# Own tiles in single buffers between long ones, x on ScalarE's queue, and g shared between two engines

## The reference

```
h   = concat([q1, q2]) @ w5 + b5                    # 300 wide
f6  = h @ w6 + b6
g   = (v @ v.T)[iu, ju]                             # all 44850 pairs i < j
f7  = (h[:, iu] * h[:, ju] * g) @ w7 + b7           # w7 is 44850 x 300
out8 = concat([f6, f7]) @ w8 + b8
y   = einsum('bu,bku->bk', out8, label_embedding)   # 200 label rows a sample
```

## Time and profile before

| | us |
|---|---|
| median of 3 runs (lowest, highest) | 1834.8 (1830.94, 1834.85) |
| the profiled execution | 1836.85 |
| its span | 1835.0 |
| PE busy | 1587.0 |
| DVE busy | 1479.3 |
| ACT busy | 921.9 |

### The profile page before, as it was taken

One profiled execution on the slowest core, in us unless ns is written; L12 is line 12 of the kernel. 1 busy time (PEld: TensorE's weight loads), 2 busy tenths in 40 slices (PEclk: granted clock), 3 DMA queues, 4 the chain that ended last, 5 costly groups with the idle time before them and its releaser, 6 DMA issues.

```text
span 1835.0 us, 24651 instructions
## 1 busy us (share of the span) xinstructions
PE 1587.0 (86%) x6936; PEld 1148.7 (63%) x6936; DVE 1479.3 (81%) x5519; ACT 921.9 (50%) x2851; POOL 33.3 (2%) x62
## 2 busy tenths in 40 slices
PE   0659999999999999997999999999999999989300
PEld 0236676777777777774777777767777777656200
DVE  8988987764699999978899987748777677498996
ACT  4443375765564646463564634434444444200798
POOL 0000000000000000000000000000000000000000
PEclk9789999999999999998999999999999999999755
DMA  7568966768789899997989999999999899899996
GB/s 283 230 262 317 368 261 247 270 216 287 290 310 419 324 401 368 384 338 303 403 306 414 344 401 409 369 304 386 353 341 344 318 387 356 273 420 421 359 417 246
DMA packets 139214, 616.99 MB, mean 336 GB/s; under 512 B 16432, under 2 KB 43693, under 8 KB 106181
## 3 DMA queue, kind: packets, MB, share of 16 engines
q1 hardware_dynamic: 105157, 368.24, 53.0%
q10 hardware_dynamic: 31744, 244.16, 34.4%
q0 software_dynamic: 2176, 3.01, 0.5%
HBM read 611.55 MB, written 3.79 MB: 335 GB/s over the span
## 4 chain that ended last, share of the span: by engine, by line
PE 71%; DVE 8%; DMA 8%; ACT 7%; SPq 3%; issue 2%; ACTq 0%; POOL 0%; DVEq 0%; POOLq 0%
PE bank L603 64%; ACT stream L753 6%; DMA wring<-in_w7p 5%; DVE junk L830 3%; PE bank L555 3%; DVE stream L946 2%; SPq L442 2%; PE bank L568 2%; DMA sring<-hrows 1%; DVE cring L928 1%; DVE cring L916 1%; ACT absjunk L669 1%; DMA stream<-in_x 1%; PE bank L544 0%; PE bank L614 0%
## 5 line engine op out<-in xcount | busy, mean ns | idle before, releaser
L603 PE MATMUL bank<-wring,cring 128*128 128x300 f32 (+1 forms) x5616 | 1451.6, 419 | 55.9 <-DVE cring L928 19.4
L603 PEld LDWEIGHTS bank<-wring,cring 128*128 128x128 f32 (+1 forms) x5616 | 1065.7, 191 | 424.4 <-DVE cring L916 30.5
L744 ACT ACTIVATE wring<-wring,gcol 128x300 f32<-128x300 f32 x1237 | 564.7, 532 | 613.3 <-DMA wring<-in_w7p 317.9
L946 DVE SCALAR_TENSOR_TENSOR stream<-stream,out 128x300 f32<-128x300 f32 x1335 | 546.0, 465 | 0.8 <-DMA stream<-in_label 0.4
L928 DVE TENSOR_TENSOR cring<-lefts,sring 128x1024 f32<-128x1024 f32 (+2 forms) x309 | 368.1, 1192 | 184.7 <-PE bank L603 182.2
L830 DVE SCALAR_TENSOR_TENSOR junk<-stream,ubc 128x300 bf16<-128x300 f32 x896 | 364.0, 465 | 10.4 <-DMA stream<-in_x 10.4
L669 ACT ACTIVATE absjunk<-stream 128x300 bf16<-128x300 f32 x448 | 196.1, 440 | 44.6 <-PE bank L603 42.6
L555 PE MATMUL bank<-stream,wts 128*32 128x300 f32 x896 | 66.2, 451 | 58.4 <-DVE small L872 58.4
L753 ACT ACTIVATE stream<-stream 128x300 f32<-128x300 f32 x265 | 115.5, 438 | 0.1
L946 DVE DVE_READ_ACCUMULATOR stream<-stream,out 128x1 f32 x1335 | 108.9, 82 | 0.0
L916 DVE SCALAR_TENSOR_TENSOR cring<-lefts,gcol,sring 128x128 f32<-128x128 f32 x334 | 95.0, 345 | 16.0 <-PE bank L603 14.8
(11 more groups left out here) (66 smaller groups left out, 241.3 us busy)
## 6 DMA issues: line engine op xcount, KB each, us to landing
stream<-in_label SPq DMA_DIRECT2D x320, 750.0 KB, 8.2
wring<-in_w7p ACTq DMA_DIRECT2D x184, 1200.0 KB, 8.4
stream<-in_x SPq DMA_DIRECT2D x64, 1050.0 KB, 12.3
sring<-hrows SPq DMA_DIRECT2D x152, 256.0 KB
wring<-in_w7p ACTq DMA_DIRECT2D x9, 1050.0 KB, 9.1
wring<-in_w7p ACTq DMA_DIRECT2D x9, 600.0 KB, 7.7
lefts<-hrows SPq DMA_DIRECT2D x48, 64.0 KB, 6.8
sring<-hrows SPq DMA_DIRECT2D x32, 88.0 KB
```

Of the source, the lines that this page charges most:

```text
L603: mm = pe.matmul(acc[b % 4][:, 0:E], cring[0:rows, p % CSLOTS, b % 2, j0 + j, :], w, start=(p == BEGIN[b] and j == 0), stop=(p == END[b] - ...
L744: ins = nc.scalar.activation(w, w, ACT.Copy, scale=gcol[:, t:t + 1])
L946: ins = nc.vector.scalar_tensor_tensor(out=row_in, in0=row_in, scalar=1.0, in1=out8[:, m % 4, :], op0=ALU.mult, op1=ALU.mult, accum_out=sc ...
```

## The change

- `unit_table` takes an order of buffers, `ORDER`. The own tiles become five units (2, 2, 2, 2 and 1 tiles), each in one buffer: the right operands in places 0 and 1, the left ones in places 2 and 3. They stand singly among A, D and B buffers. A cycle is 93 units over 24 buffers; `SHIFT` is 42. The last tile (50 rows) is now unit 74 (`SHORT`). `tile_rows` follows, so the columns of `w7p` are laid out anew.
- An own buffer is loaded by 10, 6, 6, 6 and 10 copies for each batch tile (26 in all before, 38 now).
- Single stages: of a unit's tiles, `folded(p)` (two of four, two of three, one of two, none of one) still get g on DVE, one instruction each; the others are one DVE product, and ACT scales their w7 rows. ACT's scaling therefore runs at every position. PE waits for it always.
- x loads that replace x of steps 2 and later are issued by ACT, at position `DOTS[s][1] + 5`, after `softexp` and ahead of the position's `w7_load` and `w7_scale`. Those that replace step 0 and step 1 stay on SP; those of step 1 go out at position 0, behind `s_load(0)`, `left_load(0)` and `s_load(1)` (before: position -13).
- `DOTS` is moved: step 3 has positions 0 to 18 (before -6 to 6), steps 4 and 5 end at 34 and 50 (before 24 and 43), the later ones follow. `EARLY_ROWS` goes from 65 to 80, so the tail has 64 chunks instead of 67. `STORED` goes from 5 to 7.

```
-CUSTOM = (4, 4, 1)
+CUSTOM = (2, 2, 2, 2, 1)
+ORDER = (("A", 0), ("A", 1), ("D", 0), ("A", 2), ("own", 0), ("A", 3), ("D", 1), ("A", 4), ("own", 1), ("A", 5),
+         ("D", 2), ("A", 6), ("own", 2), ("A", 7), ("own", 3), ("B", 0), ("B", 1), ("own", 4)) + tuple(
+             ("B", k) for k in range(2, NB))
...
-    SHIFT = next(k for k, u in enumerate(UNITS) if u[1] == 6)
+    SHIFT = FIRST_USE[KINDS.index(("A", 5))]
...
+    def folded(p):
+
+        n = UNITS[p % NU][3]
+        return 0 if len(live(p)) == 2 or n == 1 else min(2, n - 1)
...
-    DOTS = [(-34, -27), (-27, -20), (-20, -6), (-6, 6), (6, 24), (24, 43), (43, 54), (54, 65), (65, 77), (77, 89),
-            (100, 114), (123, 137), (146, 160), (169, 183), (192, 206), (215, 229)]
+    DOTS = [(-34, -27), (-27, -20), (-20, -4), (0, 18), (18, 34), (34, 50), (50, 60), (60, 70), (70, 80), (80, 92),
+            (105, 119), (128, 142), (151, 165), (174, 188), (197, 211), (220, 234)]
...
-    X_FREE = 7
-    STORED = 5
+    X_FREE = 5
+    L_FREE = 8
+    STORED = 7
...
-    EARLY_ROWS = 65
+    EARLY_ROWS = 80
...
+    def x_free(s):
+        return 0 if s == 1 else DOTS[s][1] + X_FREE
...
+        def x_load(queue, n):
+            if X_BEFORE[n] is not None:
+                queue.wait_ge(x_used, X_BEFORE[n] // PARTS + 1)
+            queue.dma_start(xring[:, X_SLOT[n]], x_v[n]).then_inc(x_in[X_SLOT[n]], 16)
...
-                for n in [n for n in range(XSLOTS, NS * PARTS) if DOTS[X_BEFORE[n] // PARTS][1] + X_FREE == q]:
-                    x_load(n)
                 if q == 0:
                     s_load(0)
                     left_load(0)
-                    for n in range(1, SSLOTS):
+                    s_load(1)
+                for n in [n for n in range(XSLOTS, NS * PARTS) if x_free(X_BEFORE[n] // PARTS) == q]:
+                    if X_BEFORE[n] < 2 * PARTS:
+                        x_load(sp, n)
+                if q == 0:
+                    for n in range(2, SSLOTS):
                         s_load(n)
...
-                if SHIFT <= p < SHIFT + BOTH:
-                    pe.wait_ge(w7_ready, p - SHIFT + 1)
-                else:
+                pe.wait_ge(w7_ready, p + 1)
+                if folded(p):
                     pe.wait_ge(w7_in[n_block % WSLOTS], 16 * (n_block // WSLOTS + 1))
...
-                for t in range(UNIT_TILE[u], UNIT_TILE[u + 1]):
+                for t in range(UNIT_TILE[u], UNIT_TILE[u + 1] - folded(p)):
...
+                for n in [n for n in range(XSLOTS, NS * PARTS) if x_free(X_BEFORE[n] // PARTS) == q]:
+                    if X_BEFORE[n] >= 2 * PARTS:
+                        x_load(act, n)
                 if 0 <= q < POS:
                     if q in FROM and FROM.index(q) + 2 < len(BLOCKS):
                         w7_load(FROM.index(q) + 2)
-                    if SHIFT <= q + AHEAD < SHIFT + BOTH:
+                    if q + AHEAD < POS:
                         w7_scale(q + AHEAD)
...
-                    for j in range(j0, j0 + n):
+                    b, whole = tiles[0], n - folded(p)
+                    for j in range(j0 + whole, j0 + n):
...
+                    nc.vector.tensor_tensor(cut(cring, p % CSLOTS, j0, whole), in0, cut(sring, nb % SSLOTS, j0, whole),
+                                            ALU.mult).then_inc(c_ready, 1)
```

More of the change, by code:

```diff
@@ L93, in tile_rows @@
     left[28:50], right[28:50] = 2 * P + np.arange(22), 2 * P + np.arange(22) + 22
-    tiles.append((left, right))
+    own.append((left, right))
+    tiles = []
+    for left, buf, j0, n in UNITS:
+        kind, k = KINDS[buf]
+        for j in range(j0, j0 + n):
+            if left == "own":
+                tiles.append(own[sum(CUSTOM[:k]) + j])
+            elif kind == "D":
+                tiles.append((base[left], 2 * P + 32 + (p + QUAD * k + j) % 12))
+            else:
+                tiles.append((base[left], "AB".index(kind) * P + (p + QUAD * k + j) % P))
     return np.array([t[0] for t in tiles]), np.array([t[1] for t in tiles])
 LAST_ROWS = 50
-UNITS, BUFS = unit_table()
+UNITS, KINDS = unit_table()
+BUFS = len(KINDS)
 NU = len(UNITS)
-OWN = NA + NB + ND
-LAST_USE = [max(k for k, u in enumerate(UNITS) if u[1] == b or u[0] == "own" and u[1] == b - 1) for b in range(BUFS)]
+SHORT = next(k for k, u in enumerate(UNITS) if KINDS[u[1]] == ("own", 4))
+FIRST_USE = [min(k for k, u in enumerate(UNITS) if u[1] == b) for b in range(BUFS)]
+LAST_USE = [max(k for k, u in enumerate(UNITS) if u[1] == b) for b in range(BUFS)]
 NT = sum(u[3] for u in UNITS)
@@ L143, in rec_kernel @@
     POS = END[-1]
-    BOTH = END[-2] - SHIFT
     def live(p):
@@ L778, in _ @@
                         w7_load(n)
+                if q == -1:
+                    for p in range(AHEAD):
+                        w7_scale(p)
                 for b in ended(F7_OUT, q):
@@ L909, in products @@
                 if len(tiles) == 1:
-                    b = tiles[0]
-                    for j in range(j0, j0 + n):
+                    b, whole = tiles[0], n - folded(p)
+                    cut = lambda ring, k, j, m: ring[0:rows, k, b % 2, j:j + m, :]
+                    one = left_of(left, b)[0:rows] if left != "own" else None
+                    for j in range(j0 + whole, j0 + n):
                         t = UNIT_TILE[p % NU] + j - j0
[L914 to L919, removed]
+                        nc.vector.scalar_tensor_tensor(
+                            out=cut(cring, p % CSLOTS, j, 1)[:, 0],
+                            in0=one if one is not None else cut(sring, nb % SSLOTS, j + 2, 1)[:, 0],
+                            scalar=gcol[0:rows, t:t + 1], in1=cut(sring, nb % SSLOTS, j, 1)[:, 0],
+                            op0=ALU.mult, op1=ALU.mult)
+                    in0 = (one.unsqueeze(1).to_broadcast([rows, whole, P]) if one is not None
+                           else cut(sring, nb % SSLOTS, 2, whole))
+                    nc.vector.tensor_tensor(cut(cring, p % CSLOTS, j0, whole), in0, cut(sring, nb % SSLOTS, j0, whole),
+                                            ALU.mult).then_inc(c_ready, 1)
                     return
-                cut = lambda ring, k: ring[0:rows, k, :, j0:j0 + n, :]
+                cut = lambda ring, k, j: ring[0:rows, k, :, j:j + n, :]
                 if left == "own":
-                    in0 = cut(sring, (nb + 1) % SSLOTS)
+                    in0 = cut(sring, nb % SSLOTS, 2)
                 else:
```

138 lines of the change are left out of this document (57 added, 81 removed).

## The result

The changed kernel takes 1876.5 us (median of 4 runs, 1872.37 to 1877.62) against 1834.8 before (1830.94 to 1835.33): ratio 1.0228, 95% interval 1.0207 to 1.0249. Forecast were 1859 and "slower", with a range of 1803 to 1878. The profiled execution took 1872.37 us, 1870.6 of them its span.

The account below looks back on a forecast made before the run. PE was taken to bound the kernel up to 1710 us, ACT after. PE start 104.5, first stage to 227.5, paired 1404.9, rest 227.0, plus 1.85, less 2: 1859 us, 1.3% slower; own range 1843 to 1873, whole 1803 to 1878.

Parts of the forecast that it names:

- s=9: Burst of x loads of pooling step 9 on ACT's queue, meeting seven label loads: PE stalls 8 us.
- own tiles, paired stretch: Own tiles in one buffer each: PE's 25 us idle goes, with 3 us of slow clock 28; 18 if a third stays.
- g shared: Single stages, ACT scaling part of w7 for g: 0 us, as the queue isn't empty meanwhile; bad end 20 us.
- start moved: Start: 28 rows of step 3 moved behind position 0, so PE starts at 104.5 instead of 109.9, 5.4 us gained.
- x on ACT's queue: w7 blocks land late behind x bursts: 44 us of stalls in the paired stretch, 26 in the first stage.
- six stalls of 5 to 9 us: Sign of being right: PE idles after positions 97, 125, 147, 171, 194 and 216, ended by scaling of late w7.
- short blocks: Units 66 to 69, own3 beside B0's short units: w7 block has 7.3 us, takes 8.4; 4 us over the cycles.
- rival (d): Own tiles still late because SP is full, 38 instead of 26 issues per batch tile: +10, 1869 us; chance 0.07.
- Rival (c): The w7 loop through ACT binds in the single stages as well: +20, 1879 us; chance 0.09.
- (a): x bursts on ACT's queue stay hidden, no unit is late: faster, 1805 us as a median; chance 0.22.
- (b): Half the x stalls: 20 us in the paired stretch, 20 in the first stage, 30 less: 1829 us; chance 0.17.
- End: Last single stage +1.5 us for more bytes, tail -4.4 for two shared chunks fewer; net -5, bounds -9 and +3.

Follow-up runs that it names:

- early_65: spread_g_dve with EARLY_ROWS back at 65 instead of 80: 1801.3 us, ratio 0.9806 to the kernel before.
- x_sp: The changed kernel with all x loads issued by SP again, all else kept: 1828.0 us, ratio 0.9944 to the kernel before.
- old_dots7: x_sp with g multiplied by DVE in single stages, DOTS of before and X_FREE = 7: 1821.5 us, ratio 0.9915 to the kernel before.
- spread_g_dve: The changed kernel with x_spread's order and g multiplied by DVE in the single stages: 1800.5 us, ratio 0.9812 to the kernel before.
- x_spread_again: x_spread's own code run again, beside spread_g_dve on one chip: 1820.7 us, ratio 0.9925 to the kernel before.
- x_spread: The changed kernel, x still on ACT, a burst's loads two positions apart, each behind the w7 load: 1814.4 us, ratio 0.9885 to the kernel before.

## Why the prediction was right, and where its sizes were off

| step | forecast, us | measured, us |
|---|---|---|
| DVE's first product | 99.7 | 96.8 (100.7 to 101.2 in four other traces) |
| PE's first product | 104.5 | 102.8 (107.2 to 108.0 in the same four) |
| first stage ends | 227.5 | 229.4 |
| paired stretch | 1404.9 | 1411.3 |
| last stage and tail | 227.0 | 229.9 |
| PE idle behind bursts s=2, 3, 4 | 12, 8, 6 | 11.9, 8.8, 8.5 |
| s=5, 6, 7, 8 | 0, 4, 0, 0 | 0.9, 5.4, 0, 0.9 |
| s=9 | 8 | there is no such burst |
| s=10, 12, 13 | 5.4 each | 5.4, 7.2, 6.4 |
| s=11, 14 | 8.7 each | 3.5, 1.3 |
| own tiles, paired stretch | -24 | -13 (1369.6 against 1374.9 + 8.1) |
| g shared | 0, bad end +20 | +13 and +20 by medians, +3 and +16 by the traces from PE's first product on |
| start moved | -5.4 | -6 by medians, within the noise |
| EARLY_ROWS | -4.4 of the end's -5 | about 0 (early_65) |

**x on ACT's queue.** Right in mechanism, and in the sum partly by luck: 70 us of idle forecast, 60 found, of which the trace of x_sp keeps 13. The net of the bursts is 52 us (1870.6 - 1818.7 of span).

How well the mechanism holds can be read from the landings. I gave a block 15.3 us from issue to use. The blocks behind s=10 to s=14 took 19.9, 18.2, 21.7, 20.9 and 15.1 us to land. Less 15.3 that is 4.6, 2.9, 6.4, 5.6 and 0; PE idled 5.4, 3.5, 7.2, 6.4 and 1.3. So of the six stalls of 5 to 9 us that I had named as the sign, three came. In s=11 and s=14 PE waited for an intermediate result of the pooling that ACT made behind the late block.

What was wrong in it:

- There are 12 bursts with 47 loads, not 13 of four. From step 10 on x uses only four of its nine slots, and no load replaces x of step 9, so the 8 us forecast for it could not come.
- The stall of s=4 was put in the first stage, but it fell behind it (8.5 us, at 247). That filled the place of s=9 in the paired stretch. In the first stage 6.3 us of waits for DVE's products, which the sum didn't have, filled the place of s=4. So the stages agree better than the terms do.
- I let ACT send x 4.8 us ahead of the w7 load in the one case and 1.5 us in the other; it was 7.6 (803.96 and 811.54) and 8.2, because ACT goes on to its next position as soon as it is done with the last, x waits for nothing, and the w7 load behind it waits for its slot. On the other side four x and a block took 27.4 us to land at s=10 (602.45 to about 629.9), not 25.5, and 29.3 and 28.5 at s=12 and s=13. The two cancel for s=10, 12 and 13; for s=11 and 14 the longer head start takes most of the stall away.
- PE's busy time in the paired stretch is 10.6 us longer than x_sp's, at a mean granted clock of 0.98 instead of 1.00, so some of it was at 1.2 and not at 2.4 GHz. The sum had nothing for that.

**Own tiles.** DVE's 72 us of waiting for `sring` in front of its paired products are gone altogether. But I credited PE with the whole of its 25.2 us of idle, and 14.9 were there again in old_dots7 and 13.9 in x_sp, none of them for an own tile. In old_dots7 8.2 are for the scaling of w7 (4.4 and 1.0 of it at the block behind own3) and 4.3 come after DVE waited 10.4 us for x. The short blocks are the part that I had seen and undersized: 4 us forecast, 9.3 us in spread_g_dve, and moving own3 gave 9.5. That is where rival (d) was right in size (+10) and wrong in cause: the wait was not for SP and `sring`, but for w7. The 3 us of slow clock that I took with the idle time had no row behind them; PE's busy time in x_sp is 1.9 us under 1349.7 + 8.1.

**g shared.** The step failed. I wrote that the queue isn't empty while a block is scaled, so the loop costs 0; two pairs of runs say 0.6% and 1.1%. And I looked at what ACT has room for, not at what else in its program would have to wait with it for a landing; in x_spread_again that was the larger part (8.9 against 2.4 us of PE's idle, beside 10.1 against 6.9). Rival (c) was there beside the forecast, not in its place.

**The sum.** It came out 11.2 us short: start -1.7, first stage +3.6, paired stretch +6.4, the rest +2.9. x_sp splits the two in the middle. Its first stage is 117.7 us where mine without bursts was 112 (+5.7, where g shared shows), and the bursts add 8.9 instead of 11; its paired stretch is 1369.8 against my 1360.9 (+8.9, the idle time just named), and the bursts add 41.5 instead of 44.

**Rivals (a) and (b).** (a) fell by its own mark: w7 landings of up to 21.7 us, not under 14, and 44.8 us of PE's idle in the paired stretch, not under 15. (b), 30 us less of stall than mine, fell by the 60 us found. With x_spread's order the time comes near (a)'s 1805, but stays over it: 1814 and 1821 with g shared.

**End.** The step failed, though it is small. I priced the rows that leave the tail at ACT's 2.18 us a chunk; with all of them back (early_65) the two stages together took 222.9 us against 226.0, and the medians are equal. That the DMA engines bound both is the rival's reading, and it isn't shown: their share is 1.01 in the last single stage, but 0.83 to 0.85 in the tail.

## What to carry to other kernels

A queue is also an order. Before moving transfers to another queue, list what prefetches stand behind them there, and compare the burst's time at that queue's share with the time that the prefetch has; if it is short, issue the burst in single pieces behind the prefetches, which here turned 1876 us into 1814 and 1821 (two measurements) with the same bytes in the same queue. A prefetch whose window is counted in units of work has less of it where the units are short: keep short ones apart. An engine with room is no free helper when it then stands between a landing and the next issue: list also what else is in its program behind the wait. And before counting on a burst, count the loads: which buffers are really filled again?

## What the runs showed of the hardware

With x and w7 in q10 and labels in q1, q10 got more than its half of the bytes. The 18 us from the burst of s=12 (packets, MB, share of the 16 engines):

```profile
q10 hardware_dynamic: 517, 4.09, 54.5%
q1 hardware_dynamic: 912, 3.43, 47.2%
```

and of s=10, where q1 sent many short rows for `sring` among its labels:

```profile
q10 hardware_dynamic: 650, 5.08, 76.4%
q1 hardware_dynamic: 1249, 1.43, 25.5%
```

In the five bursts of s=10 to s=14 q10 moved 224 to 287 GB/s over such 18 us, and the 245 that I used lies between. The prediction read "row by row" from one window of 5 us with 154 and 157 packets. At s=11 the counts are again nearly equal, 564 and 568, but in the two windows above, with short rows among q1's, they are not. So turns of one row each are not borne out there. The Trainium skill, "DMA: Bandwidth & Descriptors", section "Rules for kernel authors", says that spreading DMAs over issuing engines gains no bandwidth; by the trace the bytes per us indeed didn't rise (334 GB/s in the paired stretch against 338 before). What it changed here is which load stands behind which.
